# Logits of the second layer on VectorE instead of TensorE, in a two-layer graph network kernel

## The chip, the cores and the metric

The kernel runs on one core of one Trainium2 chip. The metric is device time in microseconds (us) of one launch. All times below are of that core. PE is TensorE, PEld its weight loads, DVE VectorE, ACT ScalarE, POOL GpSimd, SP SyncE.

## The reference

There are N = 6250 nodes of width D = 256 and E = 106250 edges, sorted by destination. The input is normalised by row and rectified. Then come L = 2 layers, each with K = 4 weight matrices that a softmax of four logits mixes for every node:

```python
h = relu(layernorm(x))
for l in range(2):
    logits = z @ envW[l] + envb[l]                 # (N, 4)
    weights = softmax(logits)
    agg = scatter_mean(z[col], row, N)             # mean over the edges of a node
    combined = concatenate([agg, z], axis=-1)      # (N, 512)
    outputs = einsum('nd,kdo->nko', combined, W[l]) + z[:, None, :]
    z = relu(einsum('nk,nko->no', weights, outputs))
out = x + z
```

## The kernel before

**Blocks and rounds.** The nodes lie in 49 blocks of 128. For 33 of them ("sparse") the neighbour rows are fetched: POOL gathers 128 rows at a time by index from DRAM into a ring of 12 units of two such tiles (L713), and TensorE multiplies each tile by a one-hot matrix of destinations that VectorE compares together (L869), the high and the low part of a row apart (L1329, L1334). For the other 16 ("dense") a matrix of edge counts is made in layer 1, kept in DRAM and reused in layer 2; ScalarE widens four 128x128 pieces of it at a time (`fill_stage`, L1107), and TensorE multiplies it by all 49 blocks of z, which stay in SBUF (`group_sum`, L1367, L1369, 13 groups). A layer is a first block, then 16 rounds of three slots, then an end. In each round the three slots finish the block whose sums were taken in the slot before, and take the sums of the next: **slot A** (k = 0 in the code, TensorE's `first_slot`) takes those of a sparse block, **slot B** (k = 1, `dense_slot`) those of the dense block, **slot C** (k = 2, `rest_slot`) those of a sparse block.

**The steps of one block.** VectorE adds the two parts of z (`keep_z`, L948) into `z_in`. TensorE turns it (`turn_z`, L1303), ScalarE copies it out (L1146). TensorE makes the logits, two f32 matmuls of four columns with the turned z as weights (`logits_of`, L1388; each f32 matmul is two instructions in the profile). VectorE adds the bias (L962) and takes the negated maximum (L964, both in `take_logits`), ScalarE the exponentials with their sum (L1163), VectorE the four weights (L968, L969), ScalarE scales `z_in` into `mix` (L1168). Eight products q0 to q7 follow on TensorE (L1400, f32, 512 columns, two instructions each): q0, q1, q4, q5 fill `mix_ps[0]`, and q2, q3, q6, q7 `mix_ps[1]`; q0 to q3 take the turned z and q4 to q7 the turned mean. VectorE adds the halves into `mix` with the four weights: `combine_half(0)` after q5, `combine_half(1)` after q7 (L974, two instructions each). In layer 2 `result` (L990) adds x and rectifies.

**What orders the work.** Every engine runs its own stream in the order written, and waits at semaphores. `combine_half(0)` frees `mix_ps[0]`, for which q0 of the next block waits; `result` frees `mix_ps[1]` for q2. `take_mean` (L957) waits for the sums (counted at q6) and gives the mean, which TensorE turns (L1309) and ScalarE copies (`copy_mean`, L1150) for q4. In VectorE's stream `keep_z` of the next block stands ahead of `combine_half(0)` of the present one, and it waits for the scaling of the present `z_in`. In ScalarE's stream the wait for `result` and the output's DMA (`finish`, L1180) stand ahead of the next slot's x DMA, and so ahead of its `fill_stage`, `copy_mean` and exponentials. In slot C, `look_ahead` (L899) stands between `keep_z` and `combine_half(0)`, with register work on VectorE's sequencer ahead of it. `settle` makes the DVE stream wait for the instruction just issued.

**The start of layer 2.** ScalarE issues the loads of the new weights, copies the turned z of block 0, then issues the reload of the last blocks' z (L696) and of counts. TensorE's q0 waits for the weights.

Of the kernel before, what the change touches and what calls it, by code (L numbers as in the profile page):

```python
# [5 lines left out]
P = 128  # L6
ALU = mybir.AluOpType
ACT = mybir.ActivationFunctionType
AX = mybir.AxisListType
F32 = mybir.dt.float32  # L10
# [13 lines left out]
PER_ROUND = 2  # L24
DENSE_AT = 1
WIN = 5
PAIRS_IN = (7, 6)
# [11 lines left out]
def gnn_kernel(nc, x, src, dst, W, envW, envb, out):  # L39
    N, D = x.shape  # L40
    E = src.shape[0]
    L, K, D2, _ = W.shape
    DC = D // P
# [52 lines left out]
    def sem(name):  # L96
        return ctx.enter_context(nc.semaphore(name))

    def take(eng, s, n=1):
        eng.wait_ge(s, n)  # L100
        eng.sem_inc(s, -n)  # L101

    with ctx:
# [8 lines left out]
        ident = sb("ident", [P, P])  # L112
# [95 lines left out]
        s_Tz = sem("turned_z_copied")  # L208
        s_Tm = sem("turned_mean_copied")
        s_logit = sem("logits_ready")  # L210
        s_lgfree = sem("logits_taken")
        s_nmax = sem("negmax_ready")
        s_ex = sem("exp_ready")
# [427 lines left out]
        with main_ctx:  # L641
# [4 lines left out]
            win_key = mb("win_key", [P, 2 * max(PAIRS_IN), KEYS], BF16)  # L646
            stage = mb("stage", [P, 2, STAGE, P], F32R)

            def rounds_of(eng):
                return eng.value_load(plan[0:1, RR:RR + 1], min_val=R, max_val=R_ALL)  # L650

# [47 lines left out]
            with nc.Block() as block:  # L699
# [71 lines left out]
                def _(dve):  # L771
# [173 lines left out]
                    def keep_z(blk):  # L945

                        whole = zp[:, bass.ds(blk, 1), :]
                        nc.vector.tensor_tensor(z_in[:], whole[:, :, 0:D].bitcast(F32),  # L948
                                                whole[:, :, D:2 * D].bitcast(F32), ALU.add).then_inc(s_zin, 1)

                    def take_mean(l, blk, bank):

                        take(dve, s_agg)
                        if l == 0:
# [2 lines left out]
                        nc.vector.tensor_scalar(mean[:], agg_ps[:, bank, 0:D], rcnt[:, bass.ds(blk, 1)], None,  # L957
                                                ALU.mult).then_inc(s_mean, 1)

                    def take_logits(l):  # L960
                        take(dve, s_logit)
                        settle(nc.vector.tensor_tensor(logits[:], lg_ps[:, 0:K], bias[:, l * K:(l + 1) * K], ALU.add))  # L962
                        dve.sem_inc(s_lgfree, 1)
                        nc.vector.tensor_reduce(negmax[:], logits[:], AX.X, ALU.max, negate=True).then_inc(s_nmax, 1)  # L964
# [35 lines left out]
                    for l in range(L):  # L1000
                        first = l == 0
                        zero = dve.snap(rounds * 0)
                        compare_first(sparse_block(dve, zero, 0))
                        for part in range(3):
                            compare_next(sparse_block(dve, zero, 0), part)
                        if not first:
                            dve.wait_ge(s_zload[0], 16)
                        keep_z(0)
                        compare_rest()
                        if first:  # L1010
                            make_keys()
                            window_keys(zero, 0, 0)
                            window_keys(zero, 0, 1)
                        take_mean(l, sparse_block(dve, zero, 0), 0)
                        look_ahead(sparse_block(dve, zero, 1))
                        compare_ahead()
                        compare_more()
                        if first:
                            window_keys(zero, 1, 0)
                        dve.reg_mov(table_now, zero)  # L1020
                        with dve.Fori(0, rounds) as r:
                            for k in range(ORDER):
                                take_logits(l)
                                if k == 0:
                                    compare_last(unit_no(dve.snap(next_lo)), dve.snap(next_hi))
                                    dn = nc.s_assert_within(dve.snap(table_now), 0, DENSE - 1,
                                                            skip_runtime_bounds_check_because="loaded so")
                                elif k == DENSE_AT:
                                    following = sparse_block(dve, r, k + 1)
                                    dn1 = dense_no(dve, r + 1)  # L1030
                                    compare_next(following, 0)
                                take_weights()
                                if k == DENSE_AT:
                                    compare_next(following, 1)
                                    compare_next(following, 2)
                                if first and k == 0:
                                    window_keys(dn, 1, 1)
                                elif k == 0:
                                    compare_rest()
                                if k == DENSE_AT + 1:  # L1040
                                    compare_rest()
                                if first and k:
                                    split()
                                if first and k == PER_ROUND:
                                    window_keys(dn1, 1, 0)
                                if not first and k <= DENSE_AT:
                                    for g in range(0 if k == 0 else FIRST_GROUPS, FIRST_GROUPS if k == 0 else XG):
                                        dve.wait_ge(s_zload[g], 16)
                                take(dve, s_zs)
                                keep_z(block_of(dve, r, dn, k + 1))  # L1050
                                if first and k == 0:
                                    compare_rest()
                                if first and k == DENSE_AT:
                                    window_keys(dn1, 0, 0)
                                    window_keys(dn1, 0, 1)
                                if k == PER_ROUND:
                                    more = dve.snap(r + 1)
                                    look_ahead(nc.s_assert_within(
                                        dve.snap(more * PER_ROUND + 1), 0, NB,
                                        skip_runtime_bounds_check_because="one past the last block at most"))  # L1060
                                combine_half(0)
                                take_mean(l, block_of(dve, r, dn, k + 1), bank_of(k))
                                if first and k == DENSE_AT:
                                    dve.sem_inc(s_zused, 1)
                                if k < PER_ROUND and k != DENSE_AT:
                                    compare_first(sparse_block(dve, r, k + 2 if k < DENSE_AT else k + 1))
                                elif k == PER_ROUND:
                                    with dve.If(more < rounds):
                                        compare_ahead()
                                combine_half(1)  # L1070
                                if k == PER_ROUND:
                                    with dve.If(more < rounds):
                                        compare_more()
                                if not first:
                                    result()
                            if first:
                                split()
                            dve.reg_mov(table_now, dn1)

                        take_logits(l)  # L1080
                        take_weights()
                        take(dve, s_zs)
                        combine_half(0)
                        combine_half(1)
                        if first:
                            split()
                        else:
                            result()
# [206 lines left out]
                def _(pe):  # L1295
# [77 lines left out]
                    def window_pair(j):  # L1373
# [7 lines left out]
                                           win_key[:, 2 * j + v, :], start=True, stop=True, skip_group_check=True)  # L1381
                        mm.then_inc(s_win[p], 1)

                    def logits_of(l):
                        take(pe, s_Tz)
                        take(pe, s_lgfree)
                        for c in range(DC):
                            mm = pe.matmul(lg_ps[:, 0:K], turned_z[:, c, :], envw_sb[:, l, c, :], start=(c == 0),  # L1388
                                           stop=(c == DC - 1))
                        mm.then_inc(s_logit, 1)  # L1390
                        pe.wait_ge(s_w[l], 16 * CC)

                    PRODUCTS = [(0, 0, 0), (0, 0, 1), (1, 0, 0), (1, 0, 1), (0, 1, 0), (0, 1, 1), (1, 1, 0), (1, 1, 1)]
# [141 lines left out]
                    for l in range(L):  # L1535
                        first = l == 0
                        if not first:
                            pe.sem_inc(s_free[l], RU)
                        turn_z()
                        zero = pe.snap(rounds * 0)  # L1540
                        head = header(sparse_block(pe, zero, 0))
# [50 lines left out]
```

## Time and profile before

| | us |
|---|---|
| median of 3 runs | 1765.87 |
| lowest and highest | 1763.92, 1765.96 |
| the profiled execution | 1765.67 |
| its span, first to last instruction | 1763.5 |
| mean granted TensorE clock, share of full | 0.981 |
| busy: PE, PEld | 1565.8 (89%), 1108.8 (63%) |
| busy: DVE, ACT, POOL | 886.8 (50%), 573.3 (33%), 1180.8 (67%) |

The profile is of one execution. A busy PE is not PE at its peak, since ends of matmuls are modelled and overlap; the starts tell the pace. A row of the timeline merges neighbours of one kind ("x4"), and its brackets give the idle time of the engine ahead of it and what ended it; "DVEq" or "PEq" there is the engine's own sequencer, at a semaphore or at register work. Layer 2 runs from about 931 us to the end.

### The profile page before, as it was taken

To read this page: it belongs to the slowest core of one execution; us is meant where nothing else is said; L and a number is where in the kernel's file an instruction comes from. 1 tells how busy PE (TensorE), PEld (TensorE's weight loads), DVE (VectorE), ACT (ScalarE), POOL (GpSimd) and SP (SyncE) were. 2 spreads that over 40 slices of the span, in tenths; PEclk is the share of its full clock that TensorE was granted. 3 is DMA by queue.
4 is the path that set the end of the run, shared out by engine and by line. 5 is a ranking of instruction groups with operands and counts; after the bars stand their busy time and mean duration, and the time that the engine had idled before them with its cause. 6 is when DMAs were issued, how large, how long until landed. Compare 5 with 4: busy or idle time off the path is not lost. (4 is left out here: it accounts for less than half of the span.)

```text
span 1763.5 us, 35980 instructions
## 1 busy us (share of the span) xinstructions
PE 1565.8 (89%) x8502; PEld 1108.8 (63%) x8503; DVE 886.8 (50%) x2029; ACT 573.3 (33%) x1254; POOL 1180.8 (67%) x1187
## 2 busy tenths in 40 slices
PE   1158999999999999999990899999999999999998
PEld 1036776667767777666760666676667666666665
DVE  6674665666666666566650233433433343433433
ACT  4413444444344434444340122222222222222222
POOL 1377777777777777777745776666667666666663
PEclk9989999999999999999995899999999999999999
DMA  7877777776777777767759887777777777777774
GB/s 216 278 230 222 227 226 217 214 206 205 215 215 224 213 215 224 216 209 212 204 175 381 305 246 213 214 220 213 216 228 227 214 219 220 220 221 212 223 218 146
DMA packets 160202, 393.34 MB, mean 223 GB/s; under 512 B 36989, under 2 KB 61080, under 8 KB 160180
## 3 DMA queue, kind: packets, MB, share of 16 engines
q0 software_dynamic: 92544, 302.70, 58.1%
q10 hardware_dynamic: 35112, 61.46, 9.8%
q1 hardware_dynamic: 32524, 28.91, 5.3%
q8 instruction: 11, 0.18, 0.0%
q14 instruction: 11, 0.09, 0.0%
HBM read 347.61 MB, written 45.37 MB: 223 GB/s over the span
## 5 line engine op out<-in xcount | busy, mean ns | idle before, releaser
L713 POOL DMA_INDIRECT ring<-zp_dram,gather_idx x1152 | 1162.7, 1009 | 492.9 <-issue 280.6
L1367 PE MATMUL agg_ps<-zp,stage 128*128 128x258 f32 x1568 | 447.3, 322 | 24.1 <-PEq L101 24.1
L1400 PE MATMUL mix_ps<-w_sb,turned_z 128*128 128x512 f32 x784 | 400.3, 610 | 33.2 <-PEq L101 30.9
L1329 PE MATMUL agg_ps<-ring,onehot 128*128 x1248 | 386.9, 338 | 18.6 <-PEq L101 13.7
L1400 PE MATMUL mix_ps<-w_sb,turned_m 128*128 128x512 f32 x784 | 392.5, 600 | 1.9 <-PEq L101 0.7
L1369 PE MATMUL agg_ps<-zp,stage 128*128 128x256 f32 x1568 | 384.6, 281 | 0.0
L1107 ACT ACTIVATE stage<-counts_sb 128x512 fp32r<-128x512 uint8 (+1 forms) x416 | 247.1, 605 | 388.3 <-ACTq L101 386.6
L1367 PEld LDWEIGHTS agg_ps<-zp,stage 128*128 128x128 f32 x1568 | 296.1, 189 | 88.1 <-issue 84.3
L1334 PE MATMUL agg_ps<-ring,onehot 128*128 x1248 | 320.6, 285 | 0.0
L1369 PEld LDWEIGHTS agg_ps<-zp,stage 128*128 128x128 f32 x1568 | 296.4, 189 | 34.5 <-issue 34.5
L1329 PEld LDWEIGHTS agg_ps<-ring,onehot 128*128 128x128 f32 x1248 | 238.1, 191 | 67.0 <-issue 61.7
L869 DVE TENSOR_TENSOR onehot<-nodes,dst_t 128x512 fp32r<-128x512 f32 (+1 forms) x396 | 224.1, 600 | 106.6 <-issue 92.6
L1334 PEld LDWEIGHTS agg_ps<-ring,onehot 128*128 128x128 f32 x1248 | 237.9, 191 | 29.2 <-issue 29.2
L974 DVE SCALAR_TENSOR_TENSOR mix<-mix_ps,wts,mix 128x256 f32<-128x256 f32 x392 | 188.7, 481 | 109.9 <-DVEq L101 83.5
L1400 PEld LDWEIGHTS mix_ps<-w_sb,turned_z 128*128 128x128 f32 x784 | 127.2, 193 | 75.8 <-issue 75.5
L1400 PEld LDWEIGHTS mix_ps<-w_sb,turned_m 128*128 128x128 f32 x784 | 127.0, 191 | 49.8 <-issue 47.9
L1121 ACT ACTIVATE counts_sb<-win_ps 128x490 uint8<-128x490 f32 x199 | 118.8, 597 | 110.4 <-ACTq L101 110.1
L1150 ACT ACTIVATE turned_m<-turn_ps 128x256 f32<-128x256 f32 x98 | 37.0, 378 | 336.1 <-ACTq L101 336.1
L968 DVE RECIPROCAL rsum<-ex 128x1 f32<-128x1 f32 x98 | 15.9, 162 | 252.6 <-DVEq L101 252.6
L957 DVE TENSOR_SCALAR mean<-agg_ps,rcnt 128x256 f32<-128x256 f32 x98 | 47.4, 484 | 167.4 <-DVEq L101 167.3
L940 DVE TENSOR_TENSOR win_key<-key,key_w 128x980 bf16<-128x980 f16 x67 | 120.9, 1804 | 0.0
L1380 PEld LDWEIGHTS win_ps<-win_key,win_lo 128*128 128x128 bf16 x430 | 39.1, 98 | 106.9 <-issue 103.7
(159 smaller groups left out, 897.9 us busy)
## 6 DMA issues: line engine op xcount, KB each, us to landing
ring<-zp_dram,gather_idx POOLq DMA_INDIRECT x1152, 3.8
zp_dram<-zp SPq DMA_DIRECT2D x7, 1792.0 KB, 7.1
a_dram<-counts_sb ACTq DMA_DIRECT2D x16, 784.0 KB, 5.0
zp_dram<-parts ACTq DMA_DIRECT2D x49, 256.0 KB
zp<-zp_dram SPq DMA_DIRECT2D x4, 1792.0 KB, 19.6
counts_sb<-a_dram ACTq DMA_DIRECT2D x17, 400.0 KB
parts<-in_x ACTq DMA_DIRECT2D x48, 128.0 KB
counts_sb<-a_dram ACTq DMA_DIRECT2D x16, 384.0 KB
```

The lines of the kernel that those rows point to most:

```text
L713: pool.indirect_dma_start(out=ring[:, k, t, 0:2 * D].bitcast(F32), out_offset=None, in_=zp_dram[l], in_offset=bass.IndirectOffsetOnAxis(ap ...
L869: return nc.vector.tensor_tensor(onehot[:, place:place + units, :, :].rearrange("p u t n -> p (u t) n"), nodes[:].unsqueeze(1).to_broadcas ...
L940: nc.vector.tensor_tensor(win_key[:, 2 * a:2 * b, :], key16[:].unsqueeze(1).to_broadcast([P, n, KEYS]), key_w[:, bass.ds(w, n)].unsqueeze( ...
L957: nc.vector.tensor_scalar(mean[:], agg_ps[:, bank, 0:D], rcnt[:, bass.ds(blk, 1)], None, ALU.mult).then_inc(s_mean, 1)
L974: ins = nc.vector.scalar_tensor_tensor(out=mix[:], in0=mix_ps[i][:, k * D:(k + 1) * D], scalar=wts[:, i * (K // 2) + k:i * (K // 2) + k + ...
L1107: nc.scalar.activation(stage[:, g % 2, 0:n, :], counts_sb[:, g * STAGE:g * STAGE + n, :], ACT.Copy).then_inc(s_staged, 1)
L1121: nc.scalar.activation(counts_sb[:, :, at:at + 2 * WIN].rearrange("p c (v n) -> p c v n", n=WIN), two, ACT.Copy).then_inc(s_evac, 1)
L1329: mm = pe.matmul(agg_ps[:, bank, 0:D + 2], onehot[:, place, t, :], rows[:, :, D:2 * D + 2], start=place == 0 and t == 0, stop=True, skip_g ...
L1334: mm = pe.matmul(agg_ps[:, bank, 0:D], onehot[:, place, t, :], rows[:, :, 0:D], start=False, stop=True, skip_group_check=True)
L1367: pe.matmul(agg_ps[:, bank, 0:D + 2], stage[:, g % 2, i, :], zp[:, c, D:2 * D + 2], start=c == 0, stop=True, skip_group_check=True)
L1369: mm = pe.matmul(agg_ps[:, bank, 0:D], stage[:, g % 2, i, :], zp[:, c, 0:D], start=False, stop=True, skip_group_check=True)
L1400: mm = pe.matmul(mix_ps[i][:, :], (turned_z, turned_m)[what][:, c, :], w[:, i * HALF:(i + 1) * HALF], start=what == 0 and c == 0, stop=wha ...
```

## The change

In layer 2 the two logit matmuls go. VectorE takes each logit as the sum of `z_in` times one column of the envelope weights, which must lie in all 128 partitions alike: at the start of layer 2 VectorE writes the weights on eight 128x128 diagonals, TensorE multiplies them by all ones and leaves the spread weights in `win_ps`, which layer 2 does not use otherwise. Four `scalar_tensor_tensor` with an accumulator output (`own_logits`) then stand right behind `keep_z` in slots A and B, and behind `result` in slot C; bias and maximum follow there. In both layers `keep_z` now waits until its instruction is done before the stream goes on and TensorE is told.

```diff
@@ keep_z
-                        nc.vector.tensor_tensor(z_in[:], whole[:, :, 0:D].bitcast(F32),
-                                                whole[:, :, D:2 * D].bitcast(F32), ALU.add).then_inc(s_zin, 1)
+                        settle(nc.vector.tensor_tensor(z_in[:], whole[:, :, 0:D].bitcast(F32),
+                                                       whole[:, :, D:2 * D].bitcast(F32), ALU.add))
+                        dve.sem_inc(s_zin, 1)
@@ new on VectorE
+                    def spread_weights(l):
+
+                        take(dve, s_keyfree[1])
+                        nc.vector.memset(all_ones, 1.0)
+                        for k in range(K):
+                            for c in range(DC):
+                                ins = nc.vector.tensor_scalar(diagonals[k][:, c * P:(c + 1) * P], ident[:],
+                                                              envw_sb[:, l, c, k:k + 1], None, ALU.mult)
+                        ins.then_inc(s_diag, 1)
+
+                    def own_logits(l):
+
+                        dve.wait_ge(s_spread, 1)
+                        for k in range(K):
+                            ins = nc.vector.scalar_tensor_tensor(
+                                out=terms[k], in0=z_in[:], scalar=1.0, in1=logit_weights(k),
+                                op0=ALU.mult, op1=ALU.mult, accum_out=logits[:, k:k + 1])
+                        settle(ins)
+                        settle(nc.vector.tensor_tensor(logits[:], logits[:], bias[:, l * K:(l + 1) * K], ALU.add))
+                        nc.vector.tensor_reduce(negmax[:], logits[:], AX.X, ALU.max, negate=True).then_inc(s_nmax, 1)
+
                     def take_logits(l):
+                        if l:
+                            return
@@ VectorE, first block
                         if not first:
+                            spread_weights(l)
                             dve.wait_ge(s_zload[0], 16)
                         keep_z(0)
+                        if not first:
+                            own_logits(l)
@@ VectorE, the slots
                                 keep_z(block_of(dve, r, dn, k + 1))
+                                if not first and k < PER_ROUND:
+                                    own_logits(l)
...
                                 if not first:
                                     result()
+                                if not first and k == PER_ROUND:
+                                    own_logits(l)
@@ TensorE
+                    def spread_weights():
+                        for p in range(2):
+                            take(pe, s_wfree[p])
+                        take(pe, s_diag)
+                        for k in range(K):
+                            for c in range(DC):
+                                mm = pe.matmul(logit_weights(k)[:, c * P:(c + 1) * P], all_ones,
+                                               diagonals[k][:, c * P:(c + 1) * P], start=True, stop=True,
+                                               skip_group_check=True)
+                        mm.then_inc(s_spread, 1)
+
                     def logits_of(l):
                         take(pe, s_Tz)
-                        take(pe, s_lgfree)
-                        for c in range(DC):
-                            mm = pe.matmul(lg_ps[:, 0:K], turned_z[:, c, :], envw_sb[:, l, c, :], start=(c == 0),
-                                           stop=(c == DC - 1))
-                        mm.then_inc(s_logit, 1)
+                        if l == 0:
+                            take(pe, s_lgfree)
+                            for c in range(DC):
+                                mm = pe.matmul(lg_ps[:, 0:K], turned_z[:, c, :], envw_sb[:, l, c, :], start=(c == 0),
+                                               stop=(c == DC - 1))
+                            mm.then_inc(s_logit, 1)
                         pe.wait_ge(s_w[l], 16 * CC)
@@ TensorE, first block
                             pe.sem_inc(s_free[l], RU)
+                            spread_weights()
                         turn_z()
```

The spread weights lie in PSUM; the product terms that the four instructions write besides the sum go to unused SBUF (three) and PSUM (one).

## Rows read from the trace of the kernel before

**Rows 1.** The profile's page, costliest groups: the gathers, both layers

```profile
L713 POOL DMA_INDIRECT ring<-zp_dram,gather_idx x1152 | 1162.7, 1009 | 492.9 <-issue 280.6
```

**Rows 2.** Busy time by stretch, 1180 to 1740 us: stretch, length, engines, clock, DMA

```profile
1180.00:1740.00 560.00, 539.15 (x2904) 385.48 (x2903) 214.31 (x541) 141.45 (x331) 378.63 (x401) 1.00 0.73 220
```

**Rows 3.** Instructions grouped by line, same stretch, PE: the logit matmuls

```profile
L1388 PE MATMUL lg_ps<-envw_sb,turned_z 128*128 128x4 f32 x136 | 17.2, 232 | 0.0
```

**Rows 4.** Timeline, DVE, slot A of layer 2: start, length, what

```profile
1329.06 0.42 DVE L948 TENSOR_TENSOR z_in<-zp 128x256 f32 x1 [1.14 <-DVEq L101]
1330.37 0.48 DVE L974 SCALAR_TENSOR_TENSOR mix<-mix_ps,wts,mix 128x256 f32<-128x256 f32 x1 [0.88 <-DVEq L101]
1331.00 0.48 DVE L974 SCALAR_TENSOR_TENSOR mix<-mix_ps,wts,mix 128x256 f32<-128x256 f32 x1 [0.15 <-DVEq L101]
1331.93 0.48 DVE L957 TENSOR_SCALAR mean<-agg_ps,rcnt 128x256 f32<-128x256 f32 x1 [0.44 <-DVEq L101]
...
1335.98 0.43 DVE L990 SCALAR_TENSOR_TENSOR z_out<-mix,parts 128x256 f32<-128x256 f32 x1 [0.47 <-DVEq L101]
```

**Rows 5.** Timeline, PE, same slot A and the start of slot B

```profile
1330.27 1.88 PE L1400 MATMUL mix_ps<-w_sb,turned_m 128*128 128x512 f32 x4
1331.99 0.50 PE L1388 MATMUL lg_ps<-envw_sb,turned_z 128*128 128x4 f32 x4
1332.35 1.10 PE L1400 MATMUL mix_ps<-w_sb,turned_z 128*128 128x512 f32 x2
...
1338.35 0.36 PE L1367 MATMUL agg_ps<-zp,stage 128*128 128x258 f32 x1 [1.03 <-PEq L101]
```

**Rows 6.** Timeline, ACT, start of the same slot B

```profile
1337.58 1.15 ACT L1107 ACTIVATE stage<-counts_sb 128x512 fp32r<-128x512 uint8 x2 [5.04 <-ACTq L101]
```

**Rows 7.** Timeline, slot B into slot C

```profile
1309.02 0.51 PE L1388 MATMUL lg_ps<-envw_sb,turned_z 128*128 128x4 f32 x4
...
1310.92 0.43 DVE L990 SCALAR_TENSOR_TENSOR z_out<-mix,parts 128x256 f32<-128x256 f32 x1 [0.47 <-DVEq L101]
...
1313.29 0.39 ACT L1150 ACTIVATE turned_m<-turn_ps 128x256 f32<-128x256 f32 x1 [7.47 <-ACTq L101]
...
1313.82 1.96 PE L1400 MATMUL mix_ps<-w_sb,turned_m 128*128 128x512 f32 x4
```

**Rows 8.** Timeline, end of slot C

```profile
1315.57 0.42 DVE L948 TENSOR_TENSOR z_in<-zp 128x256 f32 x1 [0.93 <-DVEq L101]
1316.84 0.29 DVE L899 TENSOR_SCALAR nodes<-lo,block_base 128x128 f32<-128x128 f16 x1 [0.85 <-issue]
1317.39 1.11 DVE L974 SCALAR_TENSOR_TENSOR mix<-mix_ps,wts,mix 128x256 f32<-128x256 f32 x2 [0.26 <-DVEq L101]
...
1318.11 0.51 PE L1388 MATMUL lg_ps<-envw_sb,turned_z 128*128 128x4 f32 x4
1318.76 1.96 PE L1400 MATMUL mix_ps<-w_sb,turned_z 128*128 128x512 f32 x4
```

**Rows 9.** Timeline, slot C's result and slot A's exponentials

```profile
1322.50 0.42 DVE L990 SCALAR_TENSOR_TENSOR z_out<-mix,parts 128x256 f32<-128x256 f32 x1
1322.84 0.15 DVE L962 TENSOR_TENSOR logits<-lg_ps,bias 128x4 f32<-128x4 f32 x1
...
1326.85 0.29 ACT L1163 ACTIVATE ex<-logits,negmax 128x4 f32<-128x4 f32 x1
1327.04 0.19 ACT L1163 ACTIVATION_READ_ACCUMULATOR ex<-logits,negmax 128x1 f32 x1
```

**Rows 10.** Timeline, layer 1: slot C's look-ahead, then slot A

```profile
569.11 0.29 DVE L899 TENSOR_SCALAR nodes<-lo,block_base 128x128 f32<-128x128 f16 x1 [0.18 <-issue]
...
581.96 0.42 DVE L948 TENSOR_TENSOR z_in<-zp 128x256 f32 x1
...
583.40 0.38 PE L1303 MATMUL turn_ps<-ident,z_in 128*128 128x128 f32 x2
```

**Rows 11.** Timeline, PE, start of layer 2: the first product

```profile
967.27 3.75 PE L1400 MATMUL mix_ps<-w_sb,turned_z 128*128 128x512 f32 x4 [30.90 <-PEq L101]
```

More of the change, by code:

```diff
@@ L210, in gnn_kernel @@
         s_logit = sem("logits_ready")
+        s_diag = sem("logit_weights_on_diagonals")
+        s_spread = sem("logit_weights_spread")
         s_lgfree = sem("logits_taken")
@@ L647, in gnn_kernel, with logit_weights @@
             stage = mb("stage", [P, 2, STAGE, P], F32R)
+            all_ones = win_lo[:].rearrange("p v n -> p (v n)")[:, 0:2 * P].bitcast(F32)
+            terms = [win_lo[:].rearrange("p v n -> p (v n)")[:, 2 * i * D:2 * (i + 1) * D].bitcast(F32) for i in range(3)]
+            terms.append(lg_ps[:, 0:D])
+            some = win_lo[:].rearrange("p v n -> p (v n)")[:, 2 * P:2 * P + 2 * (K - 1) * D].bitcast(F32)
+            diagonals = [some[:, k * D:(k + 1) * D] for k in range(K - 1)] + [mean[:]]
+            assert 2 * P + 2 * (K - 1) * D <= 2 * max(PAIRS_IN) * P and K == 4 and K * D // 2 <= 512
+            def logit_weights(k):
+                return win_ps[k // 2][:, (k % 2) * D:(k % 2 + 1) * D]
             def rounds_of(eng):
```

## The prediction

> **What bounds the kernel now.** I read the busy time by stretch first. In the steady part of layer 2 TensorE is busy 539.15 of 560 us at full granted clock, VectorE 214.31 [rows 2]. So time taken from TensorE should come back, unless TensorE's 96% hides waits. Next the gathers: one takes 1.009 us plus 280.6 / 1152 = 0.24 us of issue, 1.25 together [rows 1], while one comes every 560 / 401 = 1.40 us [rows 2]. They have 10% of room and do not bind. Then the timeline, because the busy share cannot show hidden waits. The rounds of layer 2 repeat almost to the hundredth, so one stands for 16. At every border of slots TensorE meets VectorE and ScalarE:
>
> - Slot A into B: after q6 and q7 [1330.27, rows 5] and the logits, q0 starts at 1332.35 at once. But group 2 of the dense sums starts only at 1338.35, after an idle 1.03 [rows 5]: its stage starts at 1337.58, ScalarE having waited 5.04 [rows 6] behind `result`, which VectorE starts at 1335.98 [rows 4]. So a chain q5, `combine_half(0)`, `take_mean`, compares, `combine_half(1)`, `result`, stage, group 2 already sets the pace, and it runs without pause on VectorE from 1330.37.
> - Slot B into C: q7 ends at 1309.02, `result` starts at 1310.92, `copy_mean` at 1313.29, q4 at 1313.82 [rows 7]. Between q7 and q4 TensorE has q0 to q3 and one unit, which are shorter than that chain.
> - Slot C into A: `combine_half(0)` runs 1317.39 to 1318.50, and q0 starts 0.26 later, at 1318.76, though the logits began at 1318.11 and take 0.36 elsewhere [rows 5, 8]. So q0 waits for VectorE, by 0.3.
>
> **The removed matmuls.** They are 4 instructions a block with mean 232 ns, 17.2 us busy in 34 blocks [rows 3], but overlapped. By starts they hold TensorE 1332.35 - 1331.99 = 0.36 us a block [rows 5]. For 49 blocks that is 17.6 us, or 24.8 by the busy time (17.2 / 34 = 0.51 a block). How much arrives? Into A (slot C's end), nothing: q0 waits for `combine_half(0)` anyway. Into C, nothing: q4 is set by the chain from q7. Into B, nothing, as group 2 is set by `result`. I count the gain as 0, with 17.6 as the price if all three waits were elsewhere.
>
> **Own logits, in slot A.** This is the main term. VectorE now ends `keep_z` at 1329.48 and starts `combine_half(0)` 0.88 us later [rows 4], when q5 is done. The new work stands in this gap. Its length:
> - the wait of `settle`: 0.15, as between the two L974 [rows 4];
> - four 256-column products, one operand in PSUM. The nearest is L974, 0.48 each [rows 4]. Unwaited neighbours start 0.08 before the earlier row ends (1322.50 + 0.42 against 1322.84 [rows 9]), so 0.40 each. For the accumulator output no DVE row exists. Nothing at all gives 3 x 0.40 + 0.48 = 1.68; ScalarE's own read, a separate 0.19 us row [rows 9], gives 4 x 0.59 = 2.36. VectorE's small operations start 0.07 apart if nothing waits (0.15 of L962 less 0.08 [rows 9]); I take 1.95, nearer to that;
> - settle 0.15, bias 0.15, settle 0.15, maximum about 0.10 before the next can start: 0.55.
>
> Together 0.15 + 1.95 + 0.55 = 2.65, less the 0.88 of cover: 1.8 us later (1.5 to 2.2). What is queued behind it: `combine_half(0)`, so q0 gets its bank at about 1333.5 instead of 1332.35; `take_mean`, whose 0.44 of idle [rows 4] is sequencer work, since slot C shows nearly the same, and absorbs nothing; the compares, `combine_half(1)`, `result`, and through ScalarE group 2. That already waits, so it moves by the full 1.8; q0's own 1.2 lies inside. In round 1 the gathers start cold and q5 is late, so 15 rounds count: **15 x 1.8 = 27.0** (23 to 34).
>
> The Trainium skill, "VectorE: DVE Perf Modes", section "Two Vector instructions with no wait between them", says that an operation which also writes out its accumulator is two instructions, the main one and an accumulator read. ScalarE's pair agrees; no DVE row here shows it. The same page, section "The DRAIN you can't avoid", holds that a semaphore wait between VectorE operations costs nothing over the drain; here the waited neighbour starts 0.63 after the other, the unwaited one 0.34 after [rows 4, 9]. By that rule the three settles would shrink by 0.23 each, and the term would be 15 x 1.1 = 16.
>
> **Own logits, in slots B and C.** In B `keep_z` comes early in the dense sums, and `take_mean` waits for their end, most of the slot later, so 2.7 us are covered; if that cover went, it would cost 2.7 a round. In C they follow `result`: the maximum is out 2.7 us after 1322.92, at 1325.6. The exponentials start at 1326.85 [rows 9], held by ScalarE's DMA issues, so 1.2 us of cover remain, in which `compare_last`, about 1 us, also fits. Nothing.
>
> **keep_z waits, slot C of layer 2.** Until now VectorE's sequencer did the look-ahead's register work while `keep_z` ran: L899 starts 1.27 after L948 [rows 8]. Now it begins only when `keep_z` is done, 0.42 + 0.15 later. If all 1.27 are register work, `combine_half(0)` moves by 0.57, and q0 waits for it. The lower bound is the bare wait, 0.15. The idle is ended by "issue" [rows 8], which is register work, so I take 0.55: **16 x 0.55 = 8.8** (2.4 to 9.1).
>
> **keep_z waits, layer 1.** The same look-ahead has only 0.18 idle [rows 10], because the sequencer ran ahead while VectorE was comparing; waiting puts the 1.27 behind, so L899 comes up to 1.2 later. VectorE is nearly without pause from there to `keep_z` of slot A at 581.96. TensorE turns that z at 583.40, 1.0 us after it is done [rows 10], which covers about 0.9 of 1.2. I take 0.3 a round, **16 x 0.3 = 4.8** (0 to 19 without cover).
>
> **Start and end.** Spreading is 9 small VectorE operations and 8 matmuls, at most 6 us by the turn and L899 rows at half clock. q0 waits 30.90 us there for weights [rows 11], already issued: 0, up to 6 if reloads behind it come late. In the last block the maximum is about 2 us later than now, and half is covered: **1** (0 to 2).
>
> **Sum.** 27.0 + 8.8 + 4.8 + 1 = 41.6. The profiled execution took 1765.67 (2.2 around its span), 0.2 below the median. 1765.7 + 41.6 = **1807 us**. The bounds give 1792 (23 + 2.4) to 1836 (34 + 9.1 + 19 + 2 + 6).
>
> **Rivals.**
> - *TensorE is the bound, so it gets faster.* The one point that decides: whether the new work in slot A is shorter than the 0.88 gap, or `combine_half(0)` has slack I misread. Then 49 x 0.36 = 17.6 come back: 1748. For it: 539 of 560 us busy. Against it: the 1.03 wait and the three chains. The Trainium skill, "Perfetto Trace Analysis", section "Identifying the Most-Contended Engine", says to optimise the engine of highest occupancy first, and adds that matmul busy time misjudges TensorE; its first half is this rival, its second half speaks against. Chance 0.10.
> - *It cancels.* The insertion is as good as hidden and only the settle terms are paid, against a part of the gain: 1766 give or take 4. Chance 0.06.
> - *The accumulating products take twice as long.* Each takes 0.40 more, 1.6 in all. Slot A costs 3.4 (15 x 3.4 = 51), and in C the maximum misses the exponentials with `compare_last` behind it, some 0.7 a round (11). 51 + 11 + 8.8 + 4.8 + 1 = 77: 1842. For it: no row shows one. Against it: L990 with its operands in SBUF and L974 with one in PSUM are alike, 0.43 and 0.48 [rows 4]. Chance 0.10.
> - The forecast keeps 0.74.
>
> The range 1785 to 1843 takes in the bounds, a part of the skill's cheaper wait, and the double price. About 0.2% is what a measurement here can tell from no change: faster 0.11, same 0.05, slower 0.84.
>
> **What would show it.** Right: in slot A, L974 starts about 2.6 us after `keep_z` ends; q0 of slot B comes 1.5 us after q7; the idle before group 2 is nearer 1.6 than 1.03, with TensorE waiting longer in both places; a round of layer 2 is 2.3 us longer, one of layer 1 by 0.3; in slot C L899 starts 1.8 after L948. Wrong: rounds of layer 2 shorter by about 1, or `combine_half(0)` still 0.9 after `keep_z`; layer 1 longer by more than 1 a round; products with accumulator at 0.8.

## The result, and the profile after

The changed kernel takes 1821.24 us (median of 4; 1820.72 to 1823.29) against 1765.91. The ratio is 1.0318, 95% interval 1.0302 to 1.0333. That is 55 us slower. The forecast was 1807, about 42 slower, in a range from 1785 to 1843.

The page of the kernel after: the span, and each engine's busy time.

```profile
span 1821.1 us, 36123 instructions
PE 1567.1 (86%) x8322; PEld 1087.1 (60%) x8323; DVE 971.0 (53%) x2430; ACT 573.2 (31%) x1254; POOL 1207.0 (66%) x1187
```

TensorE has 180 instructions fewer and VectorE 84 us more work, but neither number is the loss. Busy time by stretch in the steady part of layer 2 (columns as in [rows 2]; the line numbers of this kernel are 12 to 55 higher than before):

```profile
1236.00:1776.00 540.00, 487.05 (x2497) 331.86 (x2495) 253.53 (x771) 125.81 (x297) 349.65 (x364) 1.00 0.70 209
```

TensorE is now busy 90% of the stretch instead of 96%, at the same full clock. VectorE is only at 47%. So the time went into waits of TensorE, not into a full engine.

**Where it went.** `keep_z` marks every slot. Four of its rows in the timeline before: the last slot C of layer 1, block 0 and the first slot A of layer 2, and its last slot C.

```profile
912.18 0.42 DVE L948 TENSOR_TENSOR z_in<-zp 128x256 f32 x1
...
930.97 0.42 DVE L948 TENSOR_TENSOR z_in<-zp 128x256 f32<-128x256 f32 x1
...
983.15 0.43 DVE L948 TENSOR_TENSOR z_in<-zp 128x256 f32 x1 [1.14 <-DVEq L101]
...
1747.43 0.42 DVE L948 TENSOR_TENSOR z_in<-zp 128x256 f32 x1 [0.93 <-DVEq L101]
```

The same four in the timeline after:

```profile
931.44 0.42 DVE L960 TENSOR_TENSOR z_in<-zp 128x256 f32 x1
...
957.28 0.42 DVE L960 TENSOR_TENSOR z_in<-zp 128x256 f32<-128x256 f32 x1
...
1001.99 0.43 DVE L960 TENSOR_TENSOR z_in<-zp 128x256 f32 x1 [1.15 <-DVEq L101]
...
1804.49 0.42 DVE L960 TENSOR_TENSOR z_in<-zp 128x256 f32 x1 [0.92 <-DVEq L101]
```

The shifts are 19.26, 26.31, 18.84 and 57.06, of 57.6 in the span. So layer 1, whose logits did not change at all, lost 19.3. Block 0's `keep_z` came 7.05 later still (26.31 - 19.26). The spreading explains only a part of this: e4 below, which spreads but keeps layer 1 as it was, has 1.81 of it, and e1, which spreads nothing, has 5.14, nearly all of it one longer idle of VectorE ahead of the last split of layer 1 (4.59 us, where the kernel before has 0.83). e10, whose layer 1 has no waiting `keep_z`, shows that idle too (4.52); its cause is open. The wait for the weights [rows 11] covered all 7.05: the start gave 0.4 back. Layer 2's rounds lost 57.06 - 18.84 = 38.2, the end 0.5.

In these profiled executions I took the time from each `keep_z` start to the next, as the median over the rounds from the third on; the last column is the sum of the three:

| us from keep_z to keep_z | A to B | B to C | C to A | round |
|---|---|---|---|---|
| layer 1, before | 19.45 | 16.06 | 13.45 | 48.96 |
| layer 1, after | 19.12 | 16.25 | 14.87 | 50.24 |
| layer 2, before | 18.86 | 15.60 | 13.50 | 47.96 |
| layer 2, after | 20.49 | 15.59 | 14.29 | 50.37 |

**Slot A of layer 2** (+1.63). VectorE's timeline after, to compare with [rows 4]:

```profile
1365.47 0.42 DVE L960 TENSOR_TENSOR z_in<-zp 128x256 f32 x1 [1.15 <-DVEq L101]
1366.15 0.42 DVE L987 SCALAR_TENSOR_TENSOR win_lo<-z_in,win_ps 128x256 f32<-128x256 f32 x1 [0.25 <-DVEq L101]
1366.49 0.08 DVE L987 DVE_READ_ACCUMULATOR win_lo<-z_in,win_ps 128x1 f32 x1
1366.49 0.42 DVE L987 SCALAR_TENSOR_TENSOR win_lo<-z_in,win_ps 128x256 f32<-128x256 f32 x1
...
1367.52 0.14 DVE L987 DVE_READ_ACCUMULATOR lg_ps<-z_in,win_ps 128x1 f32 x1
...
1368.27 0.48 DVE L1010 SCALAR_TENSOR_TENSOR mix<-mix_ps,wts,mix 128x256 f32<-128x256 f32 x1
...
1369.84 0.48 DVE L970 TENSOR_SCALAR mean<-agg_ps,rcnt 128x256 f32<-128x256 f32 x1 [0.45 <-DVEq L101]
...
1374.03 0.43 DVE L1026 SCALAR_TENSOR_TENSOR z_out<-mix,parts 128x256 f32<-128x256 f32 x1 [0.47 <-DVEq L101]
```

`combine_half(0)` starts 2.38 us after `keep_z` ends (1368.27 - 1365.89), not 0.88: 1.50 later. (A `DVE_READ_ACCUMULATOR` row is the instruction that writes the sum out.) The 0.45 ahead of `take_mean` is still there, so it had indeed been sequencer work. What TensorE makes of it, q0 of slot B and the first matmul of group 2, against [rows 5]:

```profile
1369.80 1.10 PE L1455 MATMUL mix_ps<-w_sb,turned_z 128*128 128x512 f32 x2 [1.41 <-PEq L101]
...
1376.41 0.36 PE L1410 MATMUL agg_ps<-zp,stage 128*128 128x258 f32 x1 [1.45 <-PEq L101]
```

Two waits stand where there was one: 1.41 for the bank and 1.45 (before 1.03) for the stage, which ScalarE again fills only behind `result`:

```profile
1375.63 1.15 ACT L1150 ACTIVATE stage<-counts_sb 128x512 fp32r<-128x512 uint8 x2 [6.90 <-ACTq L101]
```

**Slot C of layer 2** (+0.79), VectorE and then TensorE's q0, against [rows 8]:

```profile
1351.18 0.42 DVE L960 TENSOR_TENSOR z_in<-zp 128x256 f32 x1 [0.92 <-DVEq L101]
1353.07 0.29 DVE L911 TENSOR_SCALAR nodes<-lo,block_base 128x128 f32<-128x128 f16 x1 [1.46 <-issue]
1353.62 1.11 DVE L1010 SCALAR_TENSOR_TENSOR mix<-mix_ps,wts,mix 128x256 f32<-128x256 f32 x2 [0.26 <-DVEq L101]
1354.98 1.95 PE L1455 MATMUL mix_ps<-w_sb,turned_z 128*128 128x512 f32 x4 [0.95 <-issue]
```

The look-ahead starts 1.89 after `keep_z` instead of 1.27: 0.62 more.

**Slot C of layer 1** (+1.42), where the forecast was worst. VectorE after:

```profile
579.15 0.42 DVE L960 TENSOR_TENSOR z_in<-zp 128x256 f32 x1
581.27 0.28 DVE L911 TENSOR_SCALAR nodes<-lo,block_base 128x128 f32<-128x128 f16 x1 [1.70 <-issue]
581.82 1.11 DVE L1010 SCALAR_TENSOR_TENSOR mix<-mix_ps,wts,mix 128x256 f32<-128x256 f32 x2 [0.26 <-DVEq L101]
```

TensorE before, at that place (q0 and q1, the mean turned, the first unit of slot A):

```profile
572.38 1.96 PE L1400 MATMUL mix_ps<-w_sb,turned_z 128*128 128x512 f32 x4
574.18 0.38 PE L1309 MATMUL turn_ps<-ident,mean 128*128 128x128 f32 x2
574.31 0.37 PE L1329 MATMUL agg_ps<-ring,onehot 128*128 x1
```

and after:

```profile
583.18 1.96 PE L1455 MATMUL mix_ps<-w_sb,turned_z 128*128 128x512 f32 x4
585.29 0.41 PE L1352 MATMUL turn_ps<-ident,mean 128*128 128x128 f32 x2
586.00 0.38 PE L1372 MATMUL agg_ps<-ring,onehot 128*128 x1 [0.31 <-PEq L101]
```

The idle ahead of the look-ahead goes from 0.18 [rows 10] to 1.70, and `combine_half(0)` runs until 582.93. Only 0.25 later q0 starts, so q0 now waits for it, if barely. From q0 to the first unit it was 1.93 us (572.38 to 574.31), now it is 2.82. Counted from the layer's `keep_z` starts (568.51 before, 579.15 after), q0 is late by 0.16 and the unit by 1.05. Layer 2 had the 2.82 before the change too (1318.76 to 1321.58 in the round of [rows 8]), and there q0 always waited. I come back to this below.

### The profile page after: what moved, and what is told of

The parts are those of the page before. It is cut to its first block and busy times, and to the rows that moved or that the text cites. A ratio compares the mean times of both kernels' runs of the same rounds, so it can differ in the third digit from the quotient of the medians.

```text
span 1821.1 us, 36123 instructions
## 1 busy us (share of the span) xinstructions
PE 1567.1 (86%) x8322; PEld 1087.1 (60%) x8323; DVE 971.0 (53%) x2430; ACT 573.2 (31%) x1254; POOL 1207.0 (66%) x1187
## 5 line engine op out<-in xcount | busy, mean ns | idle before, releaser
L725 POOL DMA_INDIRECT ring<-zp_dram,gather_idx x1152 | 1188.8, 1032 | 522.3 <-issue 283.0
L952 DVE TENSOR_TENSOR win_key<-key,key_w 128x980 bf16<-128x980 f16 x67 | 121.0, 1807 | 0.0
```

The costliest lines, as they stand in the source:

```text
L725: pool.indirect_dma_start(out=ring[:, k, t, 0:2 * D].bitcast(F32), out_offset=None, in_=zp_dram[l], in_offset=bass.IndirectOffsetOnAxis(ap ...
L952: nc.vector.tensor_tensor(win_key[:, 2 * a:2 * b, :], key16[:].unsqueeze(1).to_broadcast([P, n, KEYS]), key_w[:, bass.ds(w, n)].unsqueeze( ...
```

## The experiments

The ratios stand against runs of the kernel before on the same chip as the experiment; their medians lie between 1764.99 and 1765.95. The first four experiments take the change apart.

**e1, the waiting keep_z alone.**

```diff
-                        nc.vector.tensor_tensor(z_in[:], whole[:, :, 0:D].bitcast(F32),
-                                                whole[:, :, D:2 * D].bitcast(F32), ALU.add).then_inc(s_zin, 1)
+                        settle(nc.vector.tensor_tensor(z_in[:], whole[:, :, 0:D].bitcast(F32),
+                                                       whole[:, :, D:2 * D].bitcast(F32), ALU.add))
+                        dve.sem_inc(s_zin, 1)
```

> The kernel before with nothing but the waiting keep_z of both layers. My theory after the result: the wait costs 1.2 us a round in layer 1, because VectorE's look-ahead register work in slot C is exposed, and 0.6 to 0.8 a round in layer 2: 16 x 1.2 + 16 x 0.7 = 30 us, about 1796. Rival, the sum as predicted: 4.8 + 8.8 = 13.6, about 1780. Rival 2, a wait between VectorE operations is free: 1766.

Measured 1795.4 us, ratio 1.0171 (1.0154 to 1.0188): 29.5 slower from one wait. Its layer 1 equals the changed kernel's (slot C to A 14.85), and its layer 2 has 14.10 from C to A against 13.50, with the other two slots unchanged. So more than half of the loss has nothing to do with logits. Both rivals fall, 1780 and 1766.

**e2, the removed matmuls alone.** This kernel leaves the logits of layer 2 out, so its output is not the reference's.

```diff
                         take(pe, s_lgfree)
-                        for c in range(DC):
-                            mm = pe.matmul(lg_ps[:, 0:K], turned_z[:, c, :], envw_sb[:, l, c, :], start=(c == 0),
-                                           stop=(c == DC - 1))
-                        mm.then_inc(s_logit, 1)
+                        if l == 0:
...
+                        else:
+                            pe.sem_inc(s_logit, 1)
```

> The kernel before without the logit matmuls of layer 2; VectorE still takes the bias and the maximum of what is in the logit bank, so the weights of layer 2 are not the reference's. My theory: all three places where the time could arrive are set by VectorE and ScalarE, so it gains nothing, 1764 to 1766. Rival, TensorE is the bound: 49 x 0.36 = 17.6 us less, 1748.

Measured 1766.57, ratio 1.0007 (0.9998 to 1.0017). Taking 196 matmul instructions, with their weight loads, out of the busiest engine changed nothing, and its slots of layer 2 (18.85, 15.62, 13.51) are those of before. Where the time went is visible in one stretch of ten rounds, 1180 to 1660 us, before and in e2. TensorE's busy time falls from 461.61 to 450.51, by 11.1. Its idle time grows from 9.2 to 12.5 ahead of the group sums, from 1.5 to 4.9 ahead of the products with the turned z, and from 0.6 to 5.1 ahead of those with the turned mean: by 11.2. In a single round these are the waits ahead of group 2, q0 behind slot C and q4 of slot C, the three that the prediction had named. So every removed microsecond became a wait at one of them.

**e3, slot A's own logits behind result.**

```diff
-                                if not first and k < PER_ROUND:
+                                if not first and k == DENSE_AT:
                                     own_logits(l)
...
-                                if not first and k == PER_ROUND:
+                                if not first and k != DENSE_AT:
                                     own_logits(l)
```

> The changed kernel with slot A's own logits behind result instead of behind keep_z. My theory: the insertion ahead of combine_half(0) costs 1.66 us in 15 rounds, and behind result it is covered: 1821 - 25 = 1796. Rival, the added VectorE work costs wherever it stands (the exponentials of slot B, the compares for its units): 1815 to 1821.

Measured 1793.77, ratio 1.0157 (1.0138 to 1.0176): 27.5 of the 55 come back. Slot A to B takes 18.74, 0.12 less than before the change. The same VectorE work in another place costs nothing, and the rival (1815 to 1821) falls.

**e4, keep_z waiting in layer 2 only.** The changed kernel, whose `keep_z` takes a second argument, `not first`:

```diff
...
+                        if wait:
+                            settle(ins)
+                            dve.sem_inc(s_zin, 1)
+                        else:
+                            ins.then_inc(s_zin, 1)
...
-                                keep_z(block_of(dve, r, dn, k + 1))
+                                keep_z(block_of(dve, r, dn, k + 1), not first)
```

> The changed kernel with keep_z waiting in layer 2 only. My theory: layer 1 returns to its old rounds of 48.9 us and the 19 us come back: 1802. Rival, the prediction's 4.8 for this wait with the rest of layer 1's loss from elsewhere (the slower start, the semaphore's later signal): 1816.

Measured 1801.62, ratio 1.0208 (1.0191 to 1.0225): 19.6 come back, and layer 1's slots are 19.45, 16.06 and 13.48 again.

**e5, both mended.** e3 and e4 together, and keep_z does not wait in slots A and C of layer 2 either, since own logits now stand behind other waits there.

> The changed kernel with slot A's own logits behind result, and keep_z waiting only where own logits follow it at once (the first block and slot B of layer 2). My theory: everything that the change lost is these two things, so 1821 - 27 - 19 - 10 = about 1766, and no faster, since the freed TensorE time does not arrive. Rival, the freed time shows once the losses are gone: 1748 to 1755.

Measured 1765.96, ratio 1.0002 (0.9993 to 1.0011). The two causes account for the whole loss, and with both gone the change is worth nothing: the removed matmuls' time arrives nowhere, as in e2.

**e6 to e8, the look-ahead moved.** In slot C its register work and L899 go ahead of the wait for the scaled z.

```diff
+                                if k == PER_ROUND:
+                                    more = dve.snap(r + 1)
+                                    look_ahead(nc.s_assert_within(
...
                                 take(dve, s_zs)
                                 keep_z(block_of(dve, r, dn, k + 1))
...
-                                if k == PER_ROUND:
-                                    more = dve.snap(r + 1)
-                                    look_ahead(nc.s_assert_within(
...
                                 combine_half(0)
```

e6 does it to the kernel before:

> The kernel before with slot C's look-ahead (its register work and L899) moved ahead of the wait for the scaled z, where VectorE idles. My theory: q0 after slot C waited 0.3 us for combine_half(0) in layer 2 and not at all in layer 1, so 16 x 0.3 = 5 less, 1761. Rival, the wait had another cause: 1766; rival 2, more than q0's wait returns, up to 1.2 a round and layer: 1740 to 1750.

Measured 1764.63, ratio 0.9998 (0.9989 to 1.0007): my 5 us did not come. VectorE in its slot C:

```profile
1315.17 0.29 DVE L899 TENSOR_SCALAR nodes<-lo,block_base 128x128 f32<-128x128 f16 x1 [1.34 <-issue]
1315.85 0.49 DVE L948 TENSOR_TENSOR z_in<-zp 128x256 f32 x1 [0.40 <-DVEq L101]
```

The register work takes 1.34, and another 0.40 pass between L899 and `keep_z`, where the whole wait for the scaled z had been only 0.93 [rows 8]. So it did not fit into the wait, and it pushed `keep_z` back: B to C takes 16.72 instead of 15.60 and C to A 12.27 instead of 13.50. The gap moved from one side of `keep_z` to the other. TensorE shows the same: q0 no longer waits, and from q0 to the first unit it is 1.94 us in the median round instead of 2.82, but in the stretch from 1180 to 1660 it now idles 11.9 us ahead of `turn_z` instead of 1.1.

e7 does it to e5:

> e5 with e6's move. My theory: with VectorE's chain out of q0's way the removed matmul's 0.36 us arrives at slot C's end, and only there: 16 x (0.3 + 0.36) = 10.6 less than before, 1755. Rival, the removal brings nothing even then: as e6, 1761.

Measured 1760.17, ratio 0.9967 (0.9955 to 0.9979): 5 less than before, the first gain. It is half of what I expected, as e6's half was missing. The rival's figure, 1761, fits, but not its reason: it had the removal bring nothing beyond e6, and e7 is 4.5 below e6.

e8 does it to e1:

> e1 (waiting keep_z alone) with e6's move. My theory: the wait was dear only because the look-ahead's register work stood behind it; ahead of the wait it is covered, so the 30 us of e1 fall to at most 5: 1761 to 1768. Rival, the wait itself and the later signal to TensorE cost: 1785 to 1796.

Measured 1768.15, ratio 1.0013 (1.0004 to 1.0022). The waiting `keep_z` costs 29.5 with register work behind it and 3.5 against e6 without. So the price was not the wait, but that the sequencer cannot do its register work during the instruction that it waits for.

**e9 to e12, opening the waits.** e9, on ScalarE alone, in layer 2 of the kernel before:

```diff
-                                    for g in range(2, 4):
+                                    for g in range(2 if first else 3, 4):
                                         fill_stage(g)
...
+                                if not first and k == 0:
+                                    fill_stage(2)
                                 if not first:
                                     finish(l, blk)
```

> The kernel before with one change on ScalarE in layer 2: the third stage of dense counts is filled ahead of the wait for slot A's result. My theory: group 2 of the dense sums waited 1.2 us for it in every round and for nothing else, so 16 x 1.2 = 19 less, 1746. Rival, slot B's own chain (copied mean, weights) takes the wait's place: 1758 to 1766.

Measured 1745.66, ratio 0.9895 (0.988 to 0.991). A to B takes 17.35, 1.5 less: the wait ahead of group 2 [rows 5] is gone (no idle ahead of the group sums in the stretch from 1180 to 1660, 9.2 us before). My theory had 1746.

e10 is e7 with the same edit.

> e7 (own logits covered, early look-ahead) with e9's edit. My theory: with group 2 free, the 0.36 us of the removed matmul arrives at slot B's start as well: 1760 - 19 - 5.8 = 1735. Rival, it arrives nowhere there: 1741.

e10 measured 1734.06, ratio 0.9828 (0.9814 to 0.9841). My theory had 1735. A to B falls to 16.86, 0.49 less than in e9: the gain of the removed matmuls shows where a wait was opened. (In all it is 11.6 below e9, but the early look-ahead is in it too, and no run has that and e9's edit with the matmuls kept.)

e11 adds, in slot C of layer 2 on ScalarE (`last` is slot B's block):

```diff
+                                if not first and k == PER_ROUND:
+                                    copy_mean()
+                                    exps()
+                                    finish(l, last)
+                                last = blk
                                 if not first:
                                     fetch_x(blk)
...
                                 else:
-                                    copy_mean()
-                                    exps()
                                     scale_z(l)
                                     copy_z()
...
-                                if not first:
+                                if not first and k != DENSE_AT:
                                     finish(l, blk)
```

> e10, and in slot C ScalarE copies the turned mean and takes the exponentials ahead of the wait for slot B's result, so that q4 no longer waits for result and three DMA issues. My theory: the wait of 0.2 and the removed 0.36 arrive there too, and keep_z and combine_half(0) come about 1 us earlier: 16 x 0.6 to 1.0 less than e10, 1719 to 1725. Rival, slot C's end is then set by VectorE's look-ahead anyway: 1732 to 1735.

Measured 1706.32, ratio 0.9668 (0.9655 to 0.9681), 3.3% faster than before and 13 below the lower end of my forecast. B to C takes 14.69 instead of 16.69: 2.0 less, twice my upper figure. With the exponentials earlier `keep_z` comes earlier too: in the stretch from 1180 to 1660 TensorE idles 11.3 us ahead of `turn_z` and 5.0 ahead of q4 in e10, and 0.9 and nothing in e11. I had counted on the second wait and not on the first. The mean-first move was not run without the early look-ahead, so what each gives by itself is open.

e12 is e11 with the logits on TensorE, that is, the kernel before with the three moves:

> The kernel before, logit matmuls kept, with all three reorderings of e11. My theory: with the three waits gone TensorE is the bound, so the matmuls cost what they hold, up to 48 x 0.36 = 17 more than e11: 1736 to 1742. Rival, the matmuls are still hidden and the gain of e11 is the reordering alone: as e11 within 3.

It measured 1719.49, ratio 0.9744 (0.973 to 0.9757). So the idea of the change is worth 1719.49 - 1706.32 = 13.2 us, 0.27 a block, in a kernel where TensorE hardly waits, and nothing in the kernel that it was put in. I had expected up to 17 between the two, and 1736 to 1742 for e12, which missed because e11 came out so low; 0.27 is less than the 0.36 that the starts gave. It does not arrive alike in every slot: A to B goes from 17.43 in e12 to 17.00 in e11, B to C from 15.13 to 14.69, and C to A does not get shorter (12.28 and 12.33). What holds slot C's end there was not tried. Busy time by stretch, e11:

```profile
1150.00:1690.00 540.00, 536.96 (x2863) 382.14 (x2862) 282.86 (x860) 145.38 (x343) 404.63 (x415) 1.00 0.79 238
```

and e12:

```profile
1150.00:1710.00 560.00, 556.98 (x3036) 403.06 (x3035) 231.39 (x584) 146.94 (x348) 395.56 (x415) 1.00 0.76 231
```

TensorE is busy 99.4% in both. The kernel before had shown 96%, which looked nearly the same and was a different case.

## Why the prediction was right or wrong

**The direction and slot A: right.** "Together 0.15 + 1.95 + 0.55 = 2.65, less the 0.88 of cover: 1.8 us later." It measured 2.38 and 1.50, since the accumulating products start 0.34 apart, not 0.49. The round lost 1.63 there, which is 24.5 us in 15 rounds, and e3, which takes only this away, brought 27.5 us against my 27.0. The closeness is partly luck: 0.12 a round of it is that A to B ended below the kernel before, not at it.

**The gain counted as 0: right.** e2 shows it alone (1.0007), e5 with the losses mended (1.0002), and e2's idle times and e9 to e12 show the reason, three waits that set the borders of the slots.

**Own logits in slots B and C: nearly right.** B to C is unchanged (15.60, 15.59). In C the maximum came well ahead of the exponentials. But the weights that follow take longer:

```profile
1363.93 0.39 DVE L1005 TENSOR_SCALAR wts<-ex,rsum 128x5 f32<-128x5 f32 x1 [0.16 <-DVEq L101]
```

It is 0.39 in the median slot A and was 0.23; the rest of C to A's 0.79 beyond the look-ahead's 0.62 fits this 0.16. e5 keeps it (C to A 13.66), and in e7, with the early look-ahead, it is 0.23 again. Why it is slower was not tried.

**keep_z waits, slot C of layer 2: right** as to mechanism and nearly in size, 0.55 forecast, 0.62 measured in the look-ahead's start, 0.60 in e1's slot.

**keep_z waits, layer 1: wrong in size.** The term that failed is "which covers about 0.9 of 1.2. I take 0.3 a round, 16 x 0.3 = 4.8 (0 to 19 without cover)". It measured 19.3, and e4 shows that the wait is all of it. The two profiled executions differ by 57.6, the sum had 41.6. Of the 16.0 between them, 14.5 lie in this term and 2.4 in layer 2's rounds (38.2 against 27.0 + 8.8); the end took 0.5 less than forecast, and the start gave 0.4. (The profiled execution after, 1823.29, lies 2.05 above its median, so the medians differ from the forecast by 14.) Two errors lie in it. First, VectorE's shift was 1.5 and not 1.2: the 1.2 came from rows of layer 2, and behind the waiting `keep_z` the idle is 1.70 in layer 1 against 1.46 in layer 2. Why it is longer there was not tried. Second, I looked at one consumer, the turn of z in slot A at 583.40, and found it covered; the nearer one was q0, for which `combine_half(0)` frees the bank. The removed cover was just gone at q0, and TensorE then lost not 0.16 but 1.05 until the first unit.

The 1.05 is 0.16 at q0, 0.31 more until the mean is turned (2.11 behind q0 instead of 1.80), and 0.58 more from there to the unit. The trace offers a reason for the last two: TensorE's own sequencer has register work between q0 and the first unit of a round (the loop's end, `header`, `places`). As long as q0 does not wait, that work can be done ahead of time, and the unit starts 0.14 us after the turned mean starts in the median round of layer 1; behind a q0 that waits, it is 0.72, in layer 1 after the change as in layer 2 before and after. In e5, where q0 of layer 1 does not wait, it is 0.17, and in e6, where q0 of layer 2 does not either, 0.14. VectorE's compares, for which the units also wait, do not explain it in the round shown: the first two are done at 585.41 (start 584.39, 1.02 long), and the unit starts at 586.00. That is a reading of traces; no run took this register work away alone, so how much of the 0.89 it is stays open.

**The price of a wait.** A wait on VectorE cost what stood behind it. With it the first product starts 0.68 after `keep_z` (1366.15 - 1365.47), where an unwaited neighbour starts 0.34 after [rows 9]; e1 puts 29.5 us on such waits where register work stands behind them, and e8 against e6 3.5 where it does not. The Trainium skill, "VectorE: DVE Perf Modes", section "The DRAIN you can't avoid", holds that a semaphore between VectorE operations costs nothing extra. e1's 29.5 us go against that here. The section "Two Vector instructions with no wait between them" of the same page says that an operation which also writes out its accumulator is two instructions. The trace agrees: each product came with a `DVE_READ_ACCUMULATOR` row, and its 0.08 runs under the next product, which starts with it.

**Rivals.** "TensorE is the bound" failed at the point named: the insertion was 2.38 against 0.88. "It cancels" fell with the ratio, 1.0318. The double price fell, 0.42 a product. The upper bound of layer 1, 19, was what held.

**The signs named in advance.** Most of the signs of being right came: 2.38 against the 2.6 named in slot A, an idle of 1.45 ahead of group 2 against "nearer 1.6 than 1.03", a round of layer 2 longer by 2.41 against 2.3, the look-ahead 1.89 after `keep_z` against 1.8. One sign of being wrong came too, "layer 1 longer by more than 1 a round": it was 1.28. So the direction and layer 2 came by the mechanism that the forecast gave. In layer 1 it had the right wait and too much cover, and only its upper bound took that in. (The lower end of its bounds adds up to 1791, not 1792.)

## What to carry to other kernels

Time taken from the busiest engine arrives only where that engine's next step waits for nothing else; here three such steps waited for results behind DMA issues and other work in two in-order streams. Moving work ahead of waits in those streams gave 46 us without the change (e12), and only then did the change add 13 (e11). Put new work on an idle engine where its stream has nothing urgent behind it: ahead of `combine_half(0)` the four products and what follows them cost 27 us, behind `result` none. And count an engine's self-wait by the register work that stands behind it, in every loop that calls the helper, then follow each consumer of what gets late to the first that has no slack.

## What was not expected of the hardware

- `DVE_READ_ACCUMULATOR` takes 0.082 us (mean of 147) behind a product written to SBUF and 0.141 (49) behind the one written to PSUM, though the sum goes to SBUF in both. It adds nothing between products, since the next product starts with it.
- A wait of VectorE for its own instruction held the look-ahead up by 0.6 us in layer 2 and 1.5 in layer 1, where the sequencer had otherwise run ahead with register work. With that work moved ahead of it, the same wait cost 3.5 us in the whole kernel (e8 against e6).
- A bank that came free just too late for TensorE, 0.16 us by the starts, went with 1.05 us until the first unit of the next round.
